# Turning the rows' numbers by a DMA transpose in place of TensorE transposes, with the variance in one matmul

## What is computed

```
h   = ln(ln(x)*pw_g[path]+pw_b[path])*cp_g[kind]+cp_b[kind]
t   = ln(x)*tm_g[kind]+tm_b[kind]
s   = ln(x)*ms_g[scale]+ms_b[scale]
m,n,r = x + a row for each batch (three small MLPs of the batch's state)
cat = [w0*h, w1*t, w2*m, w3*n, w4*r, w5*s]
u   = silu(cat @ int_W1 + int_b1) @ int_W2 + int_b2
x1  = x + ln(u)*int_g + int_be
out = x1 + clip(((x1*style) @ weight.T) * dcoef + bias, -256, 256)
```

## Time and profile before

| | |
|---|---|
| time, median of 3 runs | 1160.05 us (1159.83 to 1163.53) |
| the profiled execution's own time | 1159.39 us |
| its span, first to last instruction | 1157.6 us |
| mean granted TensorE clock | 0.999 |
| busy: PE / DVE / ACT / POOL | 98% / 81% / 58% / 21% |
| busy share of the DMA engines' time, the largest queue | 25.6% |

### The profile page before, as it was taken

How to read it: one execution, slowest core, us unless ns; L and a number is a source line. 1 busy time by engine, 2 the same in 40 slices (tenths; PEclk the granted TensorE clock), 3 DMA queues, 4 the chain that set the end, 5 groups by cost and what they waited for, 6 DMA issues and landing times.

```text
span 1157.6 us, 14923 instructions
## 1 busy us (share of the span) xinstructions
PE 1137.3 (98%) x5036; PEld 925.2 (80%) x5036; DVE 933.6 (81%) x1752; ACT 676.0 (58%) x970; POOL 238.0 (21%) x268
## 2 busy tenths in 40 slices
PE   5999999999999999999999999999999999999998
PEld 4667888888888888888888888888888888888886
DVE  6898978879698787969879697896969879697836
ACT  3647475574746557375574746557375574747553
POOL 3441222213122211212212122220212212022000
PEclk9999999999999999999999999999999999999999
DMA  9953262333425233352423425333352424425001
GB/s 327 352 180 72 84 178 82 123 76 119 125 82 164 75 110 102 91 162 82 130 69 128 117 82 164 88 112 88 101 152 82 137 65 134 111 82 158 13 1 73
DMA packets 115372, 135.23 MB, mean 117 GB/s; under 512 B 69824, under 2 KB 70208, under 8 KB 115200
## 3 DMA queue, kind: packets, MB, share of 16 engines
q1 hardware_dynamic: 99872, 83.32, 25.6%
q0 software_dynamic: 14336, 50.34, 13.7%
q10 hardware_dynamic: 1088, 0.62, 0.2%
HBM read 101.74 MB, written 16.78 MB: 102 GB/s over the span
## 4 chain that ended last, share of the span: by engine, by line
PE 86%; DVE 9%; ACT 2%; issue 1%; DMA 1%; POOL 1%; SPq 0%; DVEq 0%; POOLq 0%; ACTq 0%
PE pre L1243 13%; PE pre L1247 13%; PE pre L1250 13%; PE uy L1301 5%; PE uy L1302 5%; PE uy L1304 5%; PE uy L1314 4%; PE uy L1317 4%; PE pre L1283 4%; PE uy L1315 4%; PE pre L1282 4%; PE pre L1281 4%; PE turn L1222 3%; PE pre L1264 1%; DMA ug<-x_in 1%
## 5 line engine op out<-in xcount | busy, mean ns | idle before, releaser
L435 POOL TENSOR_TENSOR ra<-vea,half 128x1 f32<-128x1 f32 x64 | 48.3, 754 | 374.9 <-DVE vea L825 374.9
L594 ACT ACTIVATE hi_a<-xT,style 128x512 fp32r<-128x512 f32 x60 | 43.5, 725 | 133.2 <-DVE xT L925 133.2
L1301 PE MATMUL uy<-hi_c,w_hi_w 128*128 128x512 f32 x256 | 101.4, 396 | 0.0
L602 ACT ACTIVATE ug<-uy,cols,dcoef 128x512 f32<-128x512 f32 x56 | 43.5, 776 | 98.5 <-PE uy L1317 98.5
L1304 PE MATMUL uy<-lo_c,w_hi_w 128*128 128x512 f32 x256 | 100.3, 392 | 0.3 <-DVE lo_c L880 0.2
L1281 PE MATMUL pre<-hi_b,w_hi_x 128*128 128x512 f32 x256 | 99.9, 390 | 0.6 <-DVE w_lo_x L1054 0.6
L1302 PE MATMUL uy<-hi_c,w_lo_w 128*128 128x512 f32 x256 | 100.0, 391 | 0.0
L1283 PE MATMUL pre<-lo_b,w_hi_x 128*128 128x512 f32 x256 | 99.7, 389 | 0.0
L1282 PE MATMUL pre<-hi_b,w_lo_x 128*128 128x512 f32 x256 | 99.6, 389 | 0.0
L857 DVE TENSOR_TENSOR lo_a<-tmp_a,hi_a 128x512 fp32r<-128x512 f32 x64 | 44.2, 690 | 66.3 <-ACT hi_a L521 66.2
L417 POOL DMA_INDIRECT gb<-pw_table,pw_ids x63 | 71.0, 1127 | 125.3 <-DMA whole_b<-gb 108.8
(11 more groups left out here) (241 smaller groups left out, 2934.1 us busy)
## 6 DMA issues: line engine op xcount, KB each, us to landing
xT<-x_turned SPq DMA_DIRECT2D x64, 256.0 KB, 2.8
out_turned<-xT SPq DMA_DIRECT2D x64, 256.0 KB, 2.0
xt<-x_in SPq DMA_DIRECT2D x62, 256.0 KB, 2.6
sel_in<-sel_ids SPq DMA_DIRECT2D x16, 192.0 KB, 2.8
raw_s<-int_w SPq DMA_DIRECT2D x2, 512.0 KB, 11.0
raw_h<-int_w SPq DMA_DIRECT2D x1, 1024.0 KB, 23.3
early_hi_w<-mlp_w SPq DMA_DIRECT2D x1, 1024.0 KB, 19.0
raw_w<-mlp_w SPq DMA_DIRECT2D x1, 1024.0 KB, 21.3
```

Of the source, the lines that this page charges most:

```text
L1301: pe.matmul(bank, w_hi["w2"][:, c, cut], hi["c"][:, c, :], start=c == 0, stop=False)
```

## The change

The four `rows_in` transposes go for groups 2 to 15. `expand_stat` writes the numbers of a tile as 16-bit halves, upper and lower apart, 256 of them, into the place of a buffer of squares. `turn_rows` is one DMA transpose for the whole group, issued by SP between the load of the first and the store of the third chunk. `join_rows` on ACT, ahead of the last `hidden`, puts the halves together, and `pick_rows` reads them from SBUF. Its place on DVE is now behind all four `low_hid`, and `first_norm` of the group's third tile goes from ahead of them to behind `low_rows`.

The sum of squares is folded on DVE from 128 to 64 partitions (`fold_sum`), its halves lie under each other in one tile of 128, and `variance` is one matmul. `rows` and the tables are 128 rows deep, rows 96 to 127 zero, filled once at the start (a memset on GpSimd, two copies on ACT). The three `gain("t", n, ...)` stand behind `unit_u` 1 to 3 and not 0 to 2. `find_root` takes `low_h` between its steps. On SP the load of the next group's first x tile goes behind two of the tile transposes. GpSimd's list has the memset in addition; otherwise no instruction in it is added, removed or moved, and it waits for what it waited for.

```diff
@@ bank_uses @@
-            uses += [("rows", i + 1)] + [("gt", i + 1, c) for c in range(3)]
+            uses += [("gt", i + 1, c) for c in range(3)]
@@ buffers @@
-        rows = sb("rows", [TROWS, GROUP], F32R)
-        tab = {n: sb(f"tab_{n}", [TROWS, D], F32R) for n in "tsb"}
+        rows = sb("rows", [P, GROUP], F32R)
+        tab = {n: sb(f"tab_{n}", [P, D], F32R) for n in "tsb"}
+        numbers_apart, numbers_turned = sq12[:, 1, :].bitcast(U16), root[:].bitcast(U16)
@@ SP @@
+            def turn_rows(i):
+                sp.wait_ge(e_ready, (i + 1) * TPG)
+                sp.wait_ge(x1_raw, (i - 1) * C)
+                sp.dma_start_transpose(numbers_turned.rearrange("p (g k) -> p g k", k=P), numbers_apart).then_inc(rows_turned, 16)
...
                         load_xT(i + 1, 0)
+                        turn_rows(i + 1)
                         store(i - 1, 2)
...
-                    if i + 2 < GROUPS:
+                    if i == 0:
                         load_xt(f + 4)
-                    if i == 0:
                         turn_tile(f + 2)
...
                         turn_tile(f)
                         turn_tile(f + 1)
+                        if i + 2 < GROUPS:
+                            load_xt(f + 4)
                         turn_tile(f + 2)
@@ ACT @@
+            def join_rows(i):
+                act.wait_ge(rows_turned, 16 * (i - 1))
+                src = numbers_turned[0:TROWS].rearrange("p (j s k) -> p j s k", j=TPG, s=2)
+                nc.scalar.activation(numbers_apart[0:TROWS].rearrange("p (j k s) -> p j s k", j=TPG, s=2), src, ACT.Copy).then_inc(rows_joined, 1)
...
-                act.wait_ge(sq_added, 3 * i + 3)
-                nc.scalar.activation(sum_r[:, 0, :], sq0[:], ACT.Copy).then_inc(sum_hi, 1)
+                act.wait_ge(sq_folded, i + 1)
+                nc.scalar.activation(sum_r[0:HALF, 0, :], sq0[0:HALF, :], ACT.Copy).then_inc(sum_hi, 1)
@@ DVE @@
+                else:
+                    src = stat[:, t % 4, :].bitcast(U16).rearrange("p (q s) -> p s q", s=2)
+                    src = src.unsqueeze(2).unsqueeze(4).to_broadcast([P, 2, 4, 4, 8])
+                    place = numbers_apart[:, t % 4 * 2 * P:(t % 4 + 1) * 2 * P]
+                    nc.vector.tensor_copy(place.rearrange("p (s n q k) -> p s n q k", s=2, n=4, q=4), src).then_inc(e_ready, 1)
...
+            def fold_sum(i):
+                dve.wait_ge(sq_added, 3 * i + 3)
+                nc.vector.tensor_tensor(sq0[0:HALF, :], sq0[0:HALF, :], sq0[HALF:P, :], ALU.add).then_inc(sq_folded, 1)
+                dve.wait_ge(sq_folded, i + 1)
@@ PE @@
-                pe.matmul(bank, vmat[:, 0:1].to_broadcast([P, P]), sum_r[:, 0, :], start=True, stop=False)
-                pe.matmul(bank, vmat[:, 0:1].to_broadcast([P, P]), sum_r[:, 1, :], start=False, stop=True).then_inc(turn_filled, 1)
+                pe.matmul(bank, vmat[:, 0:1].to_broadcast([P, P]), sum_r[:, 0, :], start=True, stop=True).then_inc(turn_filled, 1)
...
-                if more:
-                    rows_in(n)
                 for o in range(C):
                     unit_u(i, o)
-                    if more and o < 3:
-                        gain("t", n, o)
+                    if more and o > 0:
+                        gain("t", n, o - 1)
```

More of the change, by code:

```diff
@@ L25 @@
 TROWS = 3 * QUAD
+HALF = P // 2
 EPS = 1e-5
@@ L405, in _ @@
         def _(pool):
-            nc.gpsimd.memset(half[:], -0.5).then_inc(half_set, 1)
-            pool.wait_ge(half_set, 1)
+            nc.gpsimd.memset(half[:], -0.5).then_inc(consts_set, 1)
+            pool.wait_ge(consts_set, 1)
+            nc.gpsimd.memset(tmp["b"][TROWS:P, 0:2, :], 0.0).then_inc(consts_set, 1)
+            pool.wait_ge(consts_set, 2)
             def gather_gb(t):
@@ L555, in split_rows @@
                 after(act, b_used, i)
-                nc.scalar.activation(rows[:], sel_in[:].bitcast(F32), ACT.Copy).then_inc(rows_hi, 1)
+                nc.scalar.activation(rows[0:TROWS, :], sel_in[:].bitcast(F32), ACT.Copy).then_inc(rows_hi, 1)
             def hidden(i, o):
@@ L614, in _ @@
             nc.scalar.activation(vmat[:], tmp["a"][:, 0, 0:2], ACT.Copy).then_inc(vmat_ready, 1)
+            act.wait_ge(consts_set, 2)
+            nc.scalar.activation(rows[TROWS:P, :], tab_raw["t"][TROWS:P, :], ACT.Copy)
             act.wait_ge(aw_max, 1)
@@ L740, in _ @@
                     y_out(i - 1, 0)
+                add_be(i, 0)
+                if more:
                     y_out(i - 1, 1)
                     gate(n * TPG)
-                add_be(i, 0)
-                if more:
                     y_out(i - 1, 2)
                     part_halves(n * TPG)
+                    y_out(i - 1, 3)
+                hidden(i, 0)
+                if more:
                     gate(n * TPG + 1)
-                    y_out(i - 1, 3)
                     part_halves(n * TPG + 1)
[L750 to L753, removed]
+                hidden(i, 1)
+                add_be(i, 1)
+                hidden(i, 2)
+                if more:
+                    join_rows(n)
+                hidden(i, 3)
+                add_be(i, 2)
                 if more:
@@ L833, in pick_rows @@
             def pick_rows(i):
-                bank = filled(dve, "rows", i)
+                if i < 2:
+                    numbers = filled(dve, "rows", i)[0:TROWS, :]
+                else:
+                    dve.wait_ge(rows_joined, i - 1)
+                    numbers = sq12[0:TROWS, 1, :]
                 dve.wait_ge(sel_loaded, 16 * (i + 1))
-                nc.vector.scalar_tensor_tensor(out=sel_in[:].bitcast(F32), in0=sel_in[:], scalar=cmp[:, 0:1], in1=bank[0:TROWS, :],
+                nc.vector.scalar_tensor_tensor(out=sel_in[:].bitcast(F32), in0=sel_in[:], scalar=cmp[:, 0:1], in1=numbers,
                                                op0=ALU.is_equal, op1=ALU.mult).then_inc(v_done, 1)
@@ new lines, in end_root, with find_root @@
+            def end_root(v, y, h):
+                link(nc.vector.scalar_tensor_tensor(out=y, in0=h, scalar=5.0, in1=y, op0=ALU.add, op1=ALU.mult))
+                link(nc.vector.tensor_tensor(h, y, y, ALU.mult))
+                link(nc.vector.scalar_tensor_tensor(out=h, in0=h, scalar=-27.0 / 1024.0, in1=v, op0=ALU.mult, op1=ALU.mult))
+                return nc.vector.scalar_tensor_tensor(out=y, in0=h, scalar=9.0 / 16.0, in1=y, op0=ALU.add, op1=ALU.mult)
+            def find_root(i, between):
@@ L1161, in _ @@
                 low_hid(i, 2)
+                low_hid(i, 3)
                 if more:
                     pick_rows(n)
-                low_hid(i, 3)
-                if more:
                     low_rows(n)
+                    first_norm(f + 2)
+                    make_t(n, 0)
                     second_norm(f + 2)
-                    make_t(n, 0)
                     low_t(n, 0)
```

84 lines of the change are left out of this document (37 added, 47 removed).

## The result

Over four executions each, the changed kernel took 1146.54 us in the median (1145.88 to 1148.60) and the kernel before 1159.94 (1158.89 to 1163.53). The ratio is 0.9882, its 95% interval 0.9861 to 0.9902: 1.2% faster. That is 13.4 us where 9.3 were forecast, and the 1150.7 us of the prediction were 4 us too many; the measured time lies at the lowest end of its range, 1146.5. The profiled execution took 1145.88 us.

A forecast was written before the change was run, and what follows sets the result against it. TensorE, busy 98% of the span, was taken as the bound. Transposes -6.2, slow matmuls -0.3, variance -3.5, `lo_c` +0.4 and group 2 +0.3 gave -9.3 us: from 1160.05 to 1150.7 us, range 1146.5 to 1155.0.

The forecast's parts named there:

- Padding of `rows` and the tables to 128 rows ... I take nothing.: 12 matmuls in each group go from 96 to 128 rows: nothing gained, at most 3.7 us.
- the padding pays: Slow matmuls come from the change of depth between 96 and 128 and vanish: 3.7 us more, 1147.0 us; chance 0.17.
- the stall of group 2: In group 2 the numbers land late and ACT joins late: TensorE stalls about 1.1 us, net 0.3 us lost, once.
- Transposes: Four TensorE transposes ahead of `unit_u` go in 14 groups: 6.2 us, plus 0.3 us for slow matmuls behind them.
- `lo_c`: In `unit_u` the weight load for the twelfth matmul comes 0 to 0.06 us late: 0.03 x 14 = 0.4 us lost.
- Variance: One variance matmul less in 15 groups at 0.235 us each: 3.5 us gained, with `fold_sum` on DVE adding nothing.
- The join and the transfer: DMA transpose lands after 3.1 us, at worst 4.7; `join_rows` fits ACT's gap ahead of the last `hidden`: hidden.
- the covers are too thin: `lo_c`, the third gain's bank or the join come 0.1 to 0.4 us late per group: 1154.2 us; chance 0.15.
- The slower rival: Turned numbers land late, so `join_rows` holds ACT, the last `hidden` and `unit_u`: 1183 us at 8 us landing; chance 0.05.

The follow-up runs named there:

- the last kernel above: Changed kernel with the join behind the last `hidden` in group 2 alone and `unit_u`'s matmul reading the last `lo_c` three matmuls later: 1145.34 us, ratio 0.9879.

## Why the prediction was right, and where it was wrong

**The step that failed: "Padding of `rows` and the tables to 128 rows ... I take nothing."** It gives back 0.22 to 0.23 us in each group, some 3.1 us over the 14 stretches (3.3 between the medians), near the upper bound of 3.7 us that the prediction had worked out. The rival *the padding pays*, held at 0.17, was the right one. It is shown from three sides: alone (-0.19 us a group), left out (+0.23), and in a run of 48 matmuls, where 96 rows cost nothing but at the two changes. That the rival's 1147.0 us lie only 0.5 us off the measured median is in part luck: its 3.7 us were 0.5 too many, while group 2 (0.5, below) and the start (0.4, scatter) went the other way. Its 68.25 us for a group came only with the last kernel above; the changed kernel has 0.05 us of slow matmuls in `unit_u` on top.

The spans differ by 13.5 us where 9.3 were forecast. Of these 4.2 us the padding is 3.1; the stall of group 2 (0.5) and the start (0.4) make up most of the rest.

**Why the argument failed.** It ran: slow matmuls also stand behind transposes of full depth, and the variance at full depth is slow, so the cause cannot be 96 rows. But one symptom had several triggers. Behind a change of depth, in either direction, four to five matmuls stand 4 to 10 ns too far apart; behind transposes a similar lot follows; the variance matmul is itself 8 ns slow, in every kernel here; and in `unit_u` such a lot follows most of the late weight loads. That another trigger exists is no evidence against this one. The evidence was in the share: a group has 12 matmuls of depth 96 in eight places (`offsets`, and eight gains of which two stand side by side) and one place of transposes, and 0.31 us had to be shared among them. At 0.02 us for each lot, the figure that the prediction itself used for transposes, eight places come to 0.16 us; measured are 0.23. (The places are not alike: 0.04 us for `offsets`, 0.06 for the two gains side by side, 0.026 for each gain alone, and nothing more for the one right behind the variance.) The count should have decided.

The Trainium skill ("TensorE: Matmul & The Clock Gate", the table under "Why this matters for your kernels") has a matmul of depth 32 take as long as one of 128. For a matmul among its like the trace agrees (the 43 of `unit_y` at depth 96 stand 226.7 ns apart); that the change of depth has a price does not follow from it and was measured here, 0.025 us each.

**Transposes: right.** 6.2 + 0.3 - 0.4 = 6.1 us were forecast for them, the slow matmuls behind them and `lo_c` together; putting the transposes back costs 0.42 us a group, 5.9 us for 14. The estimate by the Trainium skill's gap (same page, "Back-to-back issue gap"), 0.22 us a group, is refuted by the same run.

**Variance: right.** 3.5 forecast, 15 x 0.22 = 3.3 measured, and `fold_sum` hidden. (389.13 - 388.90 is 0.23; the 0.235 that the prediction writes is the mean of the two distances in the earlier trace rows.)

**The parts and the whole.** Taken one at a time the three give 0.23 + 0.42 + 0.22 = 0.87 us of the 0.91. The difference is the lot in `unit_u`: the changed kernel pays its 0.05 us once, but it is missing in the kernel with the transposes and smaller by 0.03 us in the one with two variance matmuls, so 0.03 us count twice. The new order on DVE, ACT and SP never ran alone; what is left for it in a middle group is 0.01 us.

**`lo_c`: the size right, the form not.** The prediction had the weight load up to 0.06 us late and a wait of as much. TensorE's weight loads and matmuls in a middle group (the two engines in one stretch):

```profile
434.75 0.19 PEld L1336 LDWEIGHTS uy<-hi_c,w_lo_w 128*128 128x128 f32 x1
435.04 0.19 PEld L1338 LDWEIGHTS uy<-lo_c,w_hi_w 128*128 128x128 f32 x1
```

```profile
434.75 0.39 PE L1335 MATMUL uy<-hi_c,w_hi_w 128*128 128x512 f32 x1
434.98 0.39 PE L1336 MATMUL uy<-hi_c,w_lo_w 128*128 128x512 f32 x1
435.21 0.40 PE L1338 MATMUL uy<-lo_c,w_hi_w 128*128 128x512 f32 x1
435.45 0.40 PE L1335 MATMUL uy<-hi_c,w_hi_w 128*128 128x512 f32 x1
435.68 0.40 PE L1336 MATMUL uy<-hi_c,w_lo_w 128*128 128x512 f32 x1
435.92 0.39 PE L1338 MATMUL uy<-lo_c,w_hi_w 128*128 128x512 f32 x1
```

The load of `lo_c` starts 0.29 us behind the one ahead of it instead of 0.23: 0.06 late. The matmul that needs it does start on time to 5 ns, but from there eight matmuls are 4 to 10 ns slow, 0.05 us in all (forecast 0.03). With the matmul moved three places on, neither the late load nor the longer distances are there, and the group is 0.05 us shorter. But a late load is not enough. In the kernel with `unit_y` at 96 rows it is as late in each group from 3 on, and no matmul behind it is slow:

```profile
435.00 0.19 PEld L1336 LDWEIGHTS uy<-hi_c,w_lo_w 128*128 128x128 f32 x1
435.29 0.19 PEld L1338 LDWEIGHTS uy<-lo_c,w_hi_w 128*128 128x128 f32 x1
```

In the changed kernel itself the load comes 287 to 288 ns behind the one ahead in groups 5 to 15, with 0.053 us of slow matmuls each, and 291 to 292 ns in groups 3 and 4, with none and 0.027. So a few nanoseconds change the lot; why they do is open.

**The join and the transfer: right, with more in hand than thought.** Landing at 3.1 us, and 3.2 at worst (forecast 3.1, bound 4.7). Issue 5.9 us ahead of `unit_u` instead of 6.85. The wider copies take 0.29 us, not 0.42. The rival *the covers are too thin* is out: no wait of TensorE for the join, the rows or the bank in a middle group. The numbers are ready at 437.03 and the first gain starts at 438.20, 1.2 us later, where 0.5 + 0.3 were worked out.

**Group 2: half the stall.** ACT's timeline and TensorE's there:

```profile
157.28 0.63 ACT L581 ACTIVATE hi_c<-tmp_c 128x512 fp32r<-128x512 f32 x1
158.66 1.38 ACT L569 ACTIVATE sq<-root 96x1024 uint16<-96x1024 uint16 x1 [0.75 <-DMA root<-sq]
159.90 0.67 ACT L579 ACTIVATE tmp_c<-pre,biasc 128x512 f32<-128x512 f32 x1
```

```profile
160.88 0.39 PE L1338 MATMUL uy<-lo_c,w_hi_w 128*128 128x512 f32 x1
161.28 0.50 PE L1335 MATMUL uy<-hi_c,w_hi_w 128*128 128x512 f32 x1
161.62 0.40 PE L1336 MATMUL uy<-hi_c,w_lo_w 128*128 128x512 f32 x1
162.01 0.50 PE L1338 MATMUL uy<-lo_c,w_hi_w 128*128 128x512 f32 x1
162.34 0.39 PE L1335 MATMUL uy<-hi_c,w_hi_w 128*128 128x512 f32 x1
```

The mechanism is the one named: the transfer is late, ACT waits, the last `hidden` and `unit_u` come late. From 160.88 to 162.34 it is 1.46 us for four matmuls, 0.55 us lost and not 1.1: the join began at 158.66 and not at 159.4, the issue having gone out at 155.5. Net it is 0.2 us gained instead of 0.3 lost.

**The slower rival's mechanism is real.** From a late transfer it said "Each microsecond after 366.68 is one for TensorE"; the kernel in which `turn_rows` stands two stores and a load further back is 2.6% slower (ratio 1.0257), and its groups lose what ACT waits less 0.24 us. It did not come in because of the place in SP's queue alone. Its price was set too low: the clock adds to it.

**GpSimd.** The prediction expected nothing from its order. Its list has a memset more, and its busy time is 238.9 us where it was 238.0.

## What to carry to other kernels

When a kernel is bound by TensorE with 98% busy, divide a group's time by the number of matmuls and ask for the rest: here 0.31 us of 69.21, of which eight places with another depth held 0.23. Zero rows up to the neighbours' depth cost TensorE nothing here, since 96 rows and 128 both took 226.7 ns. When a small excess has several possible triggers, count how often each occurs and price them all; a second trigger does not clear the first. A transfer on a queue behind stores has a cliff: put it ahead of them, and read the time in hand from the trace, 1.5 us here.

## What the runs showed of the hardware that was not expected

- A change of depth between matmuls of 512 columns, 128 to 96 rows or back, puts the next four to five 4 to 10 ns further apart: 0.025 us for a change that stands alone (the kernel with `unit_y` at 96 rows), and 0.026 us for a place with one matmul of 96 rows, which has both; 0.23 us a group in eight places.
- A weight load 0.06 us late leaves the matmul that needs it on time to 5 ns. Behind it eight matmuls were 4 to 10 ns slow in 11 groups of the changed kernel, and none in the 13 middle groups of the kernel with `unit_y` at 96 rows, where it was as late.
- With the join late, TensorE fell to its 1.2 GHz level in eight of 14 groups. It had been idle for 1.8 to 4.1 us in them; of the six without a fall, five had 1.4 to 1.5 us of idle time and one 1.9. The lower level was granted from 0.3 to 1.8 us after the restart, for 3.4 us; in the group with 4.1 us of idle time from 0.9 us ahead of the restart, for 6.8 us. No run here tells what decides.
- The DMA transpose of 128x1024 16-bit numbers lands after 3.1 us in the changed kernel, and after 4.6 us (4.3 to 5.6) when it stands behind two more stores and a load.
- DVE's copy of 256 16-bit numbers a row takes 0.29 us, the one of 96 of 32 bits 0.25.
